# V's copy out of its product: from two VectorE copies to one ScalarE operation per pair of batches

## What is computed

```python
h = _modulate(_layernorm(x), shift_msa, scale_msa)
qkv = (h @ W_qkv + b_qkv).reshape(b, l, 3, H, D)      # H = 16 heads, D = 9
q, k, v = (qkv[:, :, 0], qkv[:, :, 1], qkv[:, :, 2])
attn = jax.nn.softmax(jnp.einsum('blhd,bmhd->bhlm', q * D ** (-0.5), k), axis=-1)
o = jnp.einsum('bhlm,bmhd->blhd', attn, v).reshape(b, l, c)
x = x + gate_msa * (o @ W_proj + b_proj)
```

## Time and profile before

| what | value |
|---|---|
| median of 3 runs | 1451.95 us |
| profiled execution, its own time | 1444.98 us |
| its span | 1443.2 us |
| mean granted TensorE clock | 0.955 |
| instructions in the trace | 37903 |

### The profile page before, as it was taken

How to read it: one execution, slowest core, us unless ns; L and a number is a source line. 1 busy time by engine, 2 the same in 40 slices (tenths; PEclk the granted TensorE clock), 3 DMA queues, 4 the chain that set the end, 5 groups by cost and what they waited for, 6 DMA issues and landing times.

```text
span 1443.2 us, 37903 instructions
## 1 busy us (share of the span) xinstructions
PE 1324.2 (92%) x14090; PEld 1107.0 (77%) x14090; DVE 1022.7 (71%) x2588; ACT 745.7 (52%) x1507; POOL 835.2 (58%) x2444
## 2 busy tenths in 40 slices
PE   3899999969989999998998999999889999987997
PEld 2778887758777778776887888897778887866775
DVE  7689998946568999995556545645579999875432
ACT  3357675646546767665332323332256766665441
POOL 4656656666666666566666566777777777700000
PEclk9799999989989999999999999999989999998998
DMA  5221121332351212223121212332333333301121
GB/s 150 39 16 16 18 17 15 42 90 29 31 122 15 15 15 17 15 17 62 5 13 12 13 5 14 19 29 10 28 15 23 23 24 22 21 17 17 19 44 45
DMA packets 50879, 41.93 MB, mean 29 GB/s; under 512 B 9019, under 2 KB 46318, under 8 KB 50265
## 3 DMA queue, kind: packets, MB, share of 16 engines
q0 software_dynamic: 4224, 7.45, 15.7%
q1 hardware_dynamic: 45695, 29.91, 9.4%
q10 hardware_dynamic: 780, 2.17, 0.5%
HBM read 29.14 MB, written 2.99 MB: 22 GB/s over the span
## 4 chain that ended last, share of the span: by engine, by line
PE 81%; DVE 14%; issue 2%; ACT 2%; DMA 0%; SPq 0%; ACTq 0%; DVEq 0%
PE PS L1222 17%; PE PS L1470 16%; PE PSA L1222 13%; PE PSA L1278 7%; PE PS L1302 6%; PE PS L1314 3%; DVE BIG L509 3%; PE PS L1322 3%; PE PS L1332 2%; PE PSB L1446 2%; PE PS L1333 2%; PE PSB L1222 1%; PE PS L1327 1%; DVE Q L517 1%; PE PS L1412 1%
## 5 line engine op out<-in xcount | busy, mean ns | idle before, releaser
L1083 ACT ACTIVATE BIG<-PSA 128x512 f32<-128x512 f32 (+1 forms) x224 | 131.7, 593 | 293.2 <-PE PSA L1222 293.0
L1470 PE MATMUL PS<-w,BIG 128*128 128x144 f32 (+1 forms) x1920 | 259.5, 291 | 10.9 <-DVE BIG L715 7.8
L992 ACT ACTIVATE BIG<-PSB 128x1024 f32<-128x1024 f32 x192 | 196.6, 1024 | 139.1 <-PE PSB L1285 138.5
L1470 PEld LDWEIGHTS PS<-w,BIG 128*128 128x128 f32 (+1 forms) x1920 | 250.5, 193 | 20.1 <-DVE BIG L715 8.8
L509 DVE TENSOR_REDUCE BIG<-PSA 128x8 f32<-128x1024 f32 x192 | 234.1, 1219 | 24.2 <-PE PSA L1278 20.1
L983 ACT ACTIVATE qkhi<-PS 128x512 fp32r<-128x512 f32 x188 | 112.2, 597 | 99.3 <-PE PS L1222 90.0
L1278 PE MATMUL PSA<-KK,Q 32*128 32x128 f32 x1536 | 134.8, 295 | 10.6 <-DVE Q L497 6.2
L1278 PEld LDWEIGHTS PSA<-KK,Q 32*128 32x128 f32 x1536 | 107.2, 196 | 47.0 <-issue 26.1
L1222 PE MATMUL PS<-hhi,Ahi 128*128 128x256 f32 x376 | 129.9, 346 | 8.7 <-DVE h L467 5.6
L1285 PE MATMUL PSB<-Q,KK 32*128 32x128 f32 x1536 | 132.6, 291 | 0.0
L1670 POOL MEMSET qprod<- 128x2 f32 x63 | 6.3, 101 | 212.7 <-DMA QB<-QA 212.7
(11 more groups left out here) (285 smaller groups left out, 3595.1 us busy)
## 6 DMA issues: line engine op xcount, KB each, us to landing
gate<-gates SPq DMA_DIRECT2D x96, 72.0 KB, 2.9
mgate<-gates SPq DMA_DIRECT2D x96, 72.0 KB, 2.8
X<-in_x SPq DMA_DIRECT2D x4, 576.0 KB, 14.4
out<-X SPq DMA_DIRECT2D x8, 288.0 KB, 3.7
BIG<-in_skew_w SPq DMA_DIRECT2D x2, 1024.0 KB
w<-in_w SPq DMA_DIRECT2D x1, 1440.0 KB, 7.7
BIG<-in_wqkv SPq DMA_DIRECT2D x2, 584.0 KB
BIG<-in_wm SPq DMA_DIRECT2D x1, 1154.0 KB
```

Of the source, the lines that this page charges most:

```text
L992: S.activation(PT[:, u % 2, a, :], PSB[:, :], ACT.Exp, scale=float(HD) ** -0.5).then_inc(exp_done, 1)
L1083: S.activation(hm[0:rows, slot, :], PS[(par * FTOT[l] + j) % 2][0:rows, :], gelu).then_inc(gelu_done, 1)
L1470: last = mm(o, hm[0:rows, slot, s * 128:(s + 1) * 128], w2[0:rows, FT * e + k, :], start=(k == 0), stop=(k == FT - 1))
```

## The change

`values` moves from VectorE's list to ScalarE's. There it is one operation for both batches of a pair (128 rows, 2 x 16 x 9 columns). In ScalarE's `pair(i)` it stands behind `h_high(i + 1)` and ahead of `oT_copy(o - 4)`; in the first pair of a block it also waits until `VA` has been cleared. The semaphores `v_ps` and `v_ev` keep their meaning, with ScalarE in VectorE's place. TensorE's list is as it was.

```diff
--- before
+++ after
@@ VectorE, attention(l)
-                def values(P, par):
-
-                    dve.wait_ge(v_ps, NB // 2 * l + P + 1)
-                    for s in range(2):
-                        last = V.tensor_copy(VA[:, 2 * par + s, :, 0:HD],
-                                             PS[5][:, s * C:(s + 1) * C].rearrange("p (h w) -> p h w", h=NH))
-                    last.then_inc(v_ev, 1)
...
                     if at(0):
                         row_max(e, 0)
-                        values(i, i % 2)
@@ ScalarE, attention(l)
+                def values(P, par):
+
+                    act.wait_ge(v_ps, NB // 2 * l + P + 1)
+                    S.activation(VA[:, 2 * par:2 * par + 2, :, 0:HD],
+                                 PS[5][:, 0:2 * C].rearrange("p (s h w) -> p s h w", s=2, h=NH), ACT.Copy).then_inc(v_ev, 1)
...
                     if 0 <= i + 1 < NL:
                         h_high(i + 1)
+                    if at(0):
+                        if i == 0:
+                            act.wait_ge(va_set, 2 + 2 * (l // 2))
+                        values(i, i % 2)
                     if rest:
                         rest()
                     if at(2):
                         oT_copy(o - 4, o % 2)
```

## The result

The changed kernel takes 1515.91 us (median of 4, 1510.55 to 1517.09), where the kernel before takes 1452.37 in the same session (median of 4): a ratio of 1.0431, 95% interval 1.0404 to 1.0458. That is 63.5 us slower. The forecast was 43 us slower, 1495, with a range up to 1508: the direction was right, the size too small, and the result lies beyond the range.

The account below looks back on a forecast made before the run. TensorE was taken to set the pace in the attention pairs, VectorE close behind. VectorE's relief counted 0, the delayed projection 1.03 us in 42 pairs, 43 us: 1451.95 + 43 = 1495 us, 3.0% slower, range 1483 to 1508.

Parts of the forecast that it names:

- Removed from VectorE: V's 96 copies leave VectorE, 21 us in all; gain between 0 and 0.24 us a pair, taken as 0.
- Rivals 1 and 4: VectorE's freed time: 1, key stack up to 0.24 us earlier, 1485 (chance 0.14); 4, VectorE bounds pairs, 1431 (0.04).
- Added to ScalarE: V's copy on ScalarE: 48 operations of 128x288 out of PSUM, 408 ns each, bounds 0.27 and 0.60 us.
- Moved, the wait: ScalarE's wait for V's product holds the output copies, so TensorE's projection starts late: 1.03 us in 42 pairs, 43 us.
- Does anything give it back?: Behind the late projection: scores and row maximum also 1.03 us later; out_back's delay covered, 1.8 us to spare; nothing regained.
- 1444.98 + 43: Whole kernel: the profiled execution's time plus the pairs' 43 us gives 1488; on the median's scale 1495 us.
- rival 3: TensorE in 42 pairs: the new wait alone drops the clock each time, 126 us on top, 1621; chance 0.03.
- rival 2: TensorE behind six old waits of 2.7 us or more: low clock lasts longer, 18 us more, 1513; chance 0.08.
- the dearer copy: V's copy on ScalarE at its upper bound, 0.60 us instead of 0.41: 0.19 us more a pair, 1503 us.

## Why the prediction was wrong in size, point by point

- **Removed from VectorE, taken as 0.** Right. The copy further back on ScalarE gives a ratio of 0.9998, and the reciprocal waits for out_back. Rivals 1 and 4 are out. The section Optimizing Scalar/DVE Operations of the page Perfetto Trace Analysis of the Trainium skill says that moving work off a saturated DVE to Scalar may make sense; with VectorE 91% busy in these pairs it brought nothing here even from the harmless place.
- **Added to ScalarE, 408 ns.** The line view gives 439 (438 to 443):

```profile
L979 ACT ACTIVATE VA<-PS x48: 438/439/443, 43.5 to 1342.9; 128x288 f32<-128x288 f32 x48
```

  Within the bounds, 31 ns above the value taken. The page ScalarE: Activation LUTs of the Trainium skill (section What ACT_TABLE_LOAD costs) would give 426 and comes nearer. The 30 ns are in the pair's time: from V's copy to the next start 0.33 instead of 0.30. Whether the output's runs of 9 columns cost them is not shown.
- **Moved, the wait, 1.03 us a pair.** Right, step by step: ScalarE idle 1.14 us (said 1.2), the projection's shown idle 0.82 (0.80), its first matmuls 0.51 (0.51), the pair 1.04 longer. The parts, apart: wait 0.75, copy 0.3.
- **"Does anything give it back?"** Right, nothing does. The attention output's copy ends at 214.51 + 0.58 = 215.09 (said 214.9), 1.9 us ahead of out_back at 217.01 (said 1.8).
- **The step that failed** is the sum itself: "1444.98 + 43" has no term for the clock. The prediction knew the mechanism in two forms, rivals 2 and 3, but each as something that happens everywhere (18 or 126 us more) or not at all, and put the clock at nothing: rival 3 on one row, where at 490.73 a wait of 1.01 us left the clock at 1.00, rival 2 as a small chance. The trace of the kernel before had more such rows, and they too would have misled. In that block four pairs in a row have such a wait ahead of them (0.66, 1.01, 0.74 and 0.97 us), and the clock stays at 1.00 through all of it (the last row has the columns of the earlier trace rows):

```profile
474.75 0.34 PE L1222 MATMUL PS<-Ahi,hhi 128*128 128x144 f32 x1 [0.66 <-DVE Q L517]
...
521.62 0.34 PE L1222 MATMUL PS<-Ahi,hhi 128*128 128x144 f32 x1 [0.97 <-DVE Q L517]
```

```profile
474.00:536.00 62.00, 58.16 (x805) 47.85 (x801) 59.08 (x121) 42.85 (x87) 40.18 (x111) 1.00 0.18 15
```

  Four waits that did no harm did not settle what 42 further ones do. What the runs show lies between nothing and every time: 46 to 52 us more at 1.2 GHz, about 17 to 19 us of time by the price above, some two fifths of it at the old long waits and three fifths elsewhere. The page TensorE: Matmul & The Clock Gate of the Trainium skill (section HAM oscillation) describes recurring waits that put a kernel back to the low clock. The trace agrees in part: some of the 42 waits do, most don't.
- **The range** took in the dearer copy and part of rival 2. With the clock's 19 us as a term, the sum would have been 1514. Rival 2 names 1513, near the measured 1516, but for another reason: it has 18 us at the six old waits alone.

What stays open: why one 0.82 us wait is followed by a lower clock and the next is not, since the pattern differs from one execution to the other.

## What to carry to other kernels

An operation that is moved to an engine with room brings its wait along, and in a strictly ordered queue everything behind it waits too: look first at what stands behind the new place and who needs it, then at the cost of the operation; three operations further back made 60 us of difference here. Where a change adds a recurring idle to a TensorE that runs at full clock, give the clock a term of its own, between nothing and every time, instead of a small chance for the worst. And where TensorE must stand idle for two or three microseconds ahead of dense work, matmuls that nobody reads can be worth their issue, if they fit inside the wait and the work behind isn't held by something else.

## What the runs showed of the hardware that was not expected

- Idle times of 0.82 us, 15.4 us apart, in 42 pairs, went with a fall of TensorE's mean granted clock from 0.955 to between 0.936 and 0.942, and filling them brought it to 0.964, though most of them, seen one by one, leave it at 1.00.
- A microsecond at 1.2 GHz had no single price: 0.37 us of time among the five kernels with the new wait, 0.44 to 0.53 where the old long waits were filled, 0.17 to 0.36 among the executions of the kernel before. Why it differs is open.
- 120 matmuls of 256 columns whose result nobody reads, in six waits, took the kernel from 1452.54 to 1428.8 us, with the mean granted clock at 0.968 to 0.974 instead of 0.949 to 0.962.
